# Two activation transposes moved from TensorE to transposing DMAs

## What is computed

```python
def _attn(x):
    xa = einsum('btc,dc->btd', x, W_attn + lora)          # q, k, v
    xa = (xa - xa.mean((0, 1))) * rsqrt(xa.var((0, 1)) + EPS) * bn_gamma + bn_beta
    q, k, v = split(xa, 3)
    y = softmax(causal(q @ k.T * scale)) @ v
    return (y @ W_proj.T) @ (W_proj + lora_proj).T
def _ffn(x):                                             # _bitlinear: quantised rows of x, ternary w
    return _bitlinear(silu(_bitlinear(x, w_gate)) * _bitlinear(x, w_up), w_down)
x = x + layernorm(_attn(layernorm(x)))
x = x + layernorm(_ffn(layernorm(x)))
```

## Time and profile before

| what | us |
|---|---|
| two timed runs of the kernel before | 7079.21 and 7239.78, median 7159.5 |
| the profiled execution's own time | 7071.24 |
| its span on the slowest core (core 6) | 7069.6 |
| spans of the eight cores | 7049.4 to 7069.6 |
| stage 1b, first load to last matmul | about 1801 to 2197 |
| stage 4b, first load of activations to the end | 6200 to 7070 |

### The profile page before, as it was taken

The page is one execution under the profiler, slowest core; times in us unless marked ns, Lnnn a source line. Parts: engine busy times, 40 slices in busy tenths (PEclk is TensorE's granted clock), DMA queues, the critical chain, the costliest instruction groups (busy, mean ns, idle before and its releaser), DMA issues.

```text
span 7069.6 us, 62509 instructions; the slowest of 8 cores (7049.4 to 7069.6 us)
## 1 busy us (share of the span) xinstructions
PE 4242.3 (60%) x18760; PEld 1818.9 (26%) x19100; DVE 2684.9 (38%) x3728; ACT 857.8 (12%) x1490; POOL 580.4 (8%) x2180
## 2 busy tenths in 40 slices
PE   5455555899895145555556531127777777567776
PEld 2111111223442022222222211113333333233333
DVE  2444444102443233333222234445555555542222
ACT  0222222000000001111111202111111111000000
POOL 0233333100000000000000000000000000000000
PEclk9988888999997567888888875558888888778888
DMA  4765555552222210000000023431111111222221
GB/s 138 221 192 192 191 192 192 167 177 84 72 87 72 82 35 30 30 30 23 23 23 20 21 94 126 146 125 36 36 42 39 36 36 36 92 96 75 84 84 69
DMA packets 244277, 626.46 MB, mean 89 GB/s; under 512 B 56376, under 2 KB 81000, under 8 KB 231592
## 3 DMA queue, kind: packets, MB, share of 16 engines
q1 hardware_dynamic: 243944, 622.44, 26.9%
HBM read 450.39 MB, written 171.97 MB: 88 GB/s over the span
## 4 chain that ended last, share of the span: by engine, by line
PE 45%; DVE 21%; DMA 14%; issue 10%; POOL 6%; ACT 2%; SPq 1%; DVEq 1%; POOLq 0%; another core or an unknown queue 0%; ACTq 0%
PE pall L1306 7%; PE pall L1198 5%; PE pall L680 5%; DMA xin<-x_all 5%; PE pall L1191 5%; PE pall L917 4%; PE pall L832 4%; PE pall L532 3%; DVE smalls L471 3%; DMA xt<-xnew_scr 2%; PE pall L937 2%; PE pall L538 2%; PE pall L955 2%; DMA vbn<-xa_scr 1%; POOL smalls L488 1%
## 5 line engine op out<-in xcount | busy, mean ns | idle before, releaser
L508 PE MATMUL pall<-lnx 128*128 128x512 bf16 x2007 | 606.7, 453 | 457.5 <-DVE lnx L491 454.2
L1191 PE MATMUL pall<-WgT,kqT 128*128 128x512 bf16 x1993 | 541.5, 417 | 255.3 <-DVE kqT L1180 252.1
L1198 PE MATMUL pall<-WuT,kqT 128*128 128x512 bf16 x2017 | 533.4, 409 | 98.5 <-DVE gu L1210 96.8
L1306 PE MATMUL pall<-WdT,gqT 128*128 128x512 bf16 x1990 | 507.7, 417 | 38.8 <-DVE gqT L1296 33.6
L508 PEld LDWEIGHTS pall<-lnx 128*128 128x128 bf16 x2048 | 204.3, 108 | 859.1 <-issue 725.6
L491 DVE TENSOR_SCALAR lnx<-xin,smalls 128x1024 bf16<-128x1024 f32 x256 | 208.2, 813 | 559.1 <-POOL smalls L488 559.1
L832 PE MATMUL pall<-Kfm,qfm 128*128 128x512 bf16 (+3 forms) x1136 | 286.1, 418 | 154.3 <-DVE qfm L816 153.3
L473 ACT ACTIVATE dummy1k<-xin 128x1024 f32<-128x1024 f32 x256 | 270.5, 1057 | 732.9 <-DMA xin<-x_all 732.8
L917 PE MATMUL pall<-Vtm,S_f 128*128 128x512 bf16 x1019 | 295.1, 434 | 100.8 <-DVE S_f L910 99.4
L1191 PEld LDWEIGHTS pall<-WgT,kqT 128*128 128x128 bf16 x2048 | 213.1, 105 | 533.2 <-issue 334.3
L680 PE MATMUL pall<-lnfm,WqkvT 128*128 128x512 bf16 x1504 | 343.2, 390 | 10.0 <-DVE lnfm L662 8.8
(11 more groups left out here) (213 smaller groups left out, 4630.2 us busy)
## 6 DMA issues: line engine op xcount, KB each, us to landing
xin<-x_all SPq DMA_DIRECT2D x256, 512.0 KB, 3.7
lnx_scr<-lnx SPq DMA_DIRECT2D x256, 256.0 KB, 2.2
lnb<-lnx_scr SPq DMA_DIRECT2D x256, 256.0 KB, 2.6
wstg<-w_gate SPq DMA_DIRECT2D x64, 512.0 KB, 3.6
wstg<-w_up SPq DMA_DIRECT2D x64, 512.0 KB, 4.0
gq_scr<-gq SPq DMA_DIRECT2D x32, 1024.0 KB, 4.8
gq<-gq_scr SPq DMA_DIRECT2D x32, 1024.0 KB, 6.1
xa_scr<-stg SPq DMA_DIRECT2D x48, 512.0 KB, 2.9
```

The lines of the kernel that those rows point to most:

```text
L508: s.add("pe", (lambda q, p=p, i=i, h=h, bi=bi, t=t: q.matmul(bank(bi), lnx[:, p, i * 128:(i + 1) * 128], lnx[:, p, h * 512:(h + 1) * 512], ...
L1191: s.add("pe", (lambda q, blk=blk, cj=cj, gb=gb, p=p: q.matmul(bank(gb), kqT[:, p, cj, :], WgT[:, cj, blk * 512:(blk + 1) * 512], start=(cj ...
L1198: s.add("pe", (lambda q, blk=blk, cj=cj, ub=ub, p=p: q.matmul(bank(ub), kqT[:, p, cj, :], WuT[:, cj, blk * 512:(blk + 1) * 512], start=(cj ...
L1306: s.add("pe", (lambda q, ds=ds, ic=ic, p=p: q.matmul(bank(ds), gqT[:, p, ic, :], WdT[:, ic, ds * 512:(ds + 1) * 512], start=(ic == 0), sto ...
```

## The change

The helper for DMAs gains a flag that makes the DMA transpose what it carries. In stage 1b the load `ld1b`, the 32 transposes and the 8 copies of a round are gone; 8 transposing DMAs per round, each 512 tokens x 128 channels of `lnx_scr` (128 KB), write `lnfm[:, lp, cj, :]` directly. They stand at the head of their own round, behind the six stores of the round before. In stage 4b the load `ldgq`, the 32 transposes and 4 copies of a round are gone; `ldgqT` issues 32 transposing DMAs per round, each 128 tokens x 128 channels of `gq_scr` (32 KB), into `gqT[:, p, ic, :]`. They stand where `ldgq` stood. All 8 DMAs of a round in stage 1b name the same written resource, `lnfm0` or `lnfm1`, and all 32 of a round in stage 4b name `gqT0` or `gqT1`.

```diff
-    def dma(self, eng, out, in_, reads=(), writes=(), name="dma"):
-        def emit(q, out=out, in_=in_):
+    def dma(self, eng, out, in_, reads=(), writes=(), name="dma",
+            transpose=False):
+        def emit(q, out=out, in_=in_, transpose=transpose):
+            if transpose:
+                return q.dma_start(out=out, in_=in_, transpose=True)
             return q.dma_start(out=out, in_=in_)
...
-    emit_ld1b(0)
     for st in range(8):
         lp = st % 2
         for cj in range(8):
-            tb = 2 + (cj % 2)
-            for i in range(4):
-                s.add("pe", (lambda q, i=i, cj=cj, tb=tb: q.transpose(
-                    bank_bf(tb)[:, i * 128:(i + 1) * 128],
-                    ln1b[:, i, cj * 128:(cj + 1) * 128], ident_bf)),
...
-            s.add("dve", (lambda q, cj=cj, lp=lp, tb=tb: q.tensor_copy(
-                lnfm[:, lp, cj, :], bank_bf(tb)[:, 0:512])),
-                reads=[PB[tb]], writes=[f"lnfm{lp}"], name=f"e1b{st}_{cj}")
-        if st + 1 < 8:
-            emit_ld1b(st + 1)
+            s.dma("sp", lnfm[:, lp, cj, :],
+                  lnx_scr[st * 512:(st + 1) * 512,
+                          cj * 128:(cj + 1) * 128],
+                  reads=[f"lnxs.{4 * st + i}" for i in range(4)],
+                  writes=[f"lnfm{lp}"], name=f"ldfm{st}_{cj}",
+                  transpose=True)
...
-    s.dma("sp", gq4[:, 0, :], gq_scr[0:128, :],
-          reads=["gqs.0"], writes=["gq40"], name="ldgq0")
-    transp4b(0)
+    def ldgqT(t):
+        p = t % 2
+        for ic in range(32):
+            s.dma("sp", gqT[:, p, ic, :],
+                  gq_scr[t * 128:(t + 1) * 128, ic * 128:(ic + 1) * 128],
+                  reads=[f"gqs.{t}"], writes=[f"gqT{p}"],
+                  name=f"ldgqT{t}_{ic}", transpose=True)
+
+    ldgqT(0)
     for t in range(NTO):
         if t + 1 < NTO:
-            s.dma("sp", gq4[:, (t + 1) % 2, :],
-                  gq_scr[(t + 1) * 128:(t + 2) * 128, :],
-                  reads=[f"gqs.{t + 1}"], writes=[f"gq4{(t + 1) % 2}"],
-                  name=f"ldgq{t + 1}")
+            ldgqT(t + 1)
         mm4b(t)
         tail4b(t)
-        if t + 1 < NTO:
-            transp4b(t + 1)
```

More of the change, by code:

```diff
@@ L654, in _build @@
         for cj in range(8):
-            tb = 2 + (cj % 2)
-            for i in range(4):
-                s.add("pe", (lambda q, i=i, cj=cj, tb=tb: q.transpose(
-                    bank_bf(tb)[:, i * 128:(i + 1) * 128],
-                    ln1b[:, i, cj * 128:(cj + 1) * 128], ident_bf)),
-                    reads=["R_xin0", "R_xin1", "R_xin2", "R_xin3", "ident_bf"],
-                    writes=[PB[tb]], name=f"t1b{st}_{cj}_{i}")
-            s.add("dve", (lambda q, cj=cj, lp=lp, tb=tb: q.tensor_copy(
-                lnfm[:, lp, cj, :], bank_bf(tb)[:, 0:512])),
-                reads=[PB[tb]], writes=[f"lnfm{lp}"], name=f"e1b{st}_{cj}")
-        if st + 1 < 8:
-            emit_ld1b(st + 1)
+            s.dma("sp", lnfm[:, lp, cj, :],
[4 more added lines that the diff above has]
+                  transpose=True)
         if dbg and st == 0:
```

## The result

The changed kernel takes 9055.5 us in the median of 11 runs, 8918 to 9215; the kernel before, measured again beside it, 7097.8 in the median of 10. The ratio is 1.263, 95% interval 1.258 to 1.267: slower by a quarter. The profiled execution took 8920.2 us, against 7071.2 of the one before, +1849 us. The eight cores lie between 8887 and 8919 us, where they lay between 7049 and 7070. In some executions the cores of one die run at a lower granted clock than the others; where that was so in an experiment, cores of the other die are named.

What follows compares the result with a forecast made beforehand. SP's chain of transposing round trips was taken to bound both stages, no longer PE, DVE or the clock: 7071.2 + 1905 (stage 4b) + 266 (stage 1b) = 9242, given as 9240 us, range 8500 to 10,400.

Steps and rivals of the forecast that it cites:

- d, a step of 32 KB: Stage 4b, one chained round trip of a 32 KB transposing DMA: 2.55 us, middle of plain 2.0 and piece-wise 3.1.
- residual, store and back, per round: Stage 4b, after a round's last transposing issue: residual's load, two DVE operations, store, next issue: 7.1 us.
- the last matmuls and the tail: End of stage 4b: last matmuls 13.6 us, 3.75 for low clock, 9.4 after the last PSUM reading: 27 us.
- stage 4b: SP's chain of 32 loads, then residual and store, sets a round of 86 us where it was 26.3: +1905 us.
- D, a step of 128 KB: Stage 1b, one chained round trip of a 128 KB transposing DMA: 4.6 us, middle of plain 2.5 and piece-wise 6.8.
- the low clock after the longer gaps: Stage 1b, the low clock may hold 7.5 us after a turn's gap, not 3: 2.2 us per turn.
- stage 1b: Eight 128 KB round trips exposed at the start and each turn, behind the stores: 294 - 28 = +266 us.
- The cover of the matmuls: Stage 4b: matmuls, 30 us even wholly at low clock, plus 8 us of tail fit into 79 us of next loads.
- B: Both stages: transposing costs nothing beyond the plain load, steps of 2.0 and 2.5 us, total 8560 us; 20%.
- D (about 30 ms): Both stages: transposition element by element in two-byte pieces, 17 us per 32 KB, about 30 ms; 4%.
- C: Both stages: SP's issue is slow as well, 1.4 us more: 11,410 us with the pieces, 10,040 without; 17%.
- A: Stage 4b: the 32 loads go out together at 0.33 us per issue, a round about 21 us, total 6905; 1%.

Runs made afterwards that it cites:

- experiment 2: The changed kernel with plain DMAs of the same slices in place of transposing ones, still chained, the transposition left out: span 8428.6 us.
- experiment 3: The changed kernel with one transposing DMA of 1 MB per round in each stage, in place of 32 and 8: span 6754.0 us, ratio 0.957 to the kernel before.
- experiment 1: The changed kernel with every slice of gqT and lnfm a resource of its own, so no transposing DMA waits for the one before: span 7803.6 us.
- experiment 10: Against experiment 9: stage 4b's transposing DMA of round t+2 issued right after round t's matmuls, ahead of residual's load and store: span 6639.1 us, ratio 0.939.
- experiment 7: The changed kernel, chains kept, with stage 1b's DMAs ahead of the stores and stage 4b's residual load ahead of the 32 DMAs: 8690 to 8703 us, cores 0 to 3.
- experiments 8 and 9: 8: against experiment 3, stage 1b's load ahead of stores, stage 4b's residual load ahead: 6720.2 us (core 3). 9: against 8, residual's load behind again: 6668.0 us.

## Why the prediction held, and where its sizes were off

The sign, the mechanism and the order of stages held: SP's chain, 1024 + 64 round trips, sets the end of both stages. The forecast of 9240 stands 184 above the median and 320 above the profiled execution, on which its terms rest: +2169 us were forecast and +1849 measured. Step by step:

| step | predicted | measured | worth |
|---|---|---|---|
| d, a step of 32 KB | 2.55 (2.0 to 3.1) | 2.33 | 994 x 0.22 = 219 us too much |
| residual, store and back, per round | 7.1 | 7.5 | 12 us too little |
| the last matmuls and the tail | 27 | 25.1 (8893.5 to 8918.6) | 2 too much |
| stage 4b | +1905 | +1698 | |
| D, a step of 128 KB | 4.6 (2.5 to 6.8) | 2.73 | 64 x 1.87 = 120 too much |
| the low clock after the longer gaps | 7 x 2.2 = 15 | 351.6 - 344.5 = 7 | 8 too much |
| stage 1b | +266 | +139 | |

**d.** Both of its halves were a little off, and in the same direction. The plain step is 1.85 us (experiment 2) where the chain of pA gave 2.0: that chain ran through TensorE and DVE between its loads, this one through SP alone. The transposition costs 0.48, where the middle of the two bounds gave 0.55. That this comes so close is luck: the 0.55 is half the price of pieces that the runs do not show, as D makes plain.

**D.** The step that failed is the assumption behind the upper end, that the transposition goes by pieces of 32 bytes at 16.7 ns of one DMA engine each. Four times the pieces cost 0.30 us more than a plain load and not 4.3. The counts of packets say the same (DMA of 7001 to 7053 us of the changed kernel, 23 issues to `gqT`, and of 7006 to 7058 us of experiment 2, 29 issues: packets, MB, share of 16 engines):

```profile
q1 hardware_dynamic: 3624, 0.74, 6.6%
...
q1 hardware_dynamic: 4106, 0.94, 7.8%
```

A transposing DMA of 32 KB has about 158 packets and a plain one 142; there are no 1024 packets for the assumed 1024 pieces. The term was sized from the packet price of a plain DMA and had no row of its own; with the 0.48 of d in its place D would have been 2.5 + 0.5.

**Stage 4b's round.** The order came out as written: L(t+1), residual, store, L(t+2), with L1337 waiting for the residual. What I had not seen is that a transposing DMA holds SP for 1.09 us, so that the residual's issue comes 1.14 us after the last one and not 0.45; its landing in 3.6 us instead of 3.8 made up for little of that. The cover of the matmuls was ample: they take 15.6 us of a round, and not for much of it at the low clock, as I had written, but for 3.1 us.

**Stage 1b.** The gap is 1.45 + 8 D as composed, and its mean of 23.3 gives the D of 2.73. The clock cost less than the 2.2 us a turn that I allowed: the matmuls of a round took 0.9 us longer in the mean than in the kernel before.

**What three rules of the Trainium skill give.** By "VectorE: DVE Perf Modes" of the Trainium skill, section on the three transpose paths, with its 1309 ns on top of the plain chain, d would have been 3.3; it is 2.33, and against the plain chain as measured here the transposition adds 0.48. By "Advanced Engine Details and Errata" of the Trainium skill, section X-Bar Transpose, it would cost nothing; the rows say 0.48 us per DMA of 32 KB and 1.1 us of SP instead of 0.32. What the runs bear out is the rule of "DMA: Bandwidth & Descriptors" of the Trainium skill, in its rules for kernel authors, to coalesce many small transfers because those under 64 KB are mostly overhead: experiment 3 moves what 32 DMAs of 32 KB moved in one, and its span is 2165 us below that of the changed kernel.

**The rivals.** B (8560, 20%) is refuted by experiment 2: the transposition has a price. Without it the same chains take 8429 us, below B's sum, since the plain step is 1.85 us and not 2.0. D (about 30 ms) is out by the measured step of 2.33 us. C was right that the issue is slower, by 0.77 us and not 1.4, but wrong on what that costs a chain: the step grows by 0.48 us in all, so part of the slow issue hides in the round trip; it comes to light in full when the chain is taken away (experiment 1). A was priced with the issue of a plain DMA, 0.33 us. With the true 1.29 its round is 48 us, so independent DMAs of 32 KB would not have ended on the other side. The way to a faster kernel was none of the rivals: fewer and larger DMAs.

## What to carry to other kernels

Before a DMA replaces on-chip work, count the round trips that its queue makes in a row: a scheduler that tracks a tile by one name turns n loads into a chain of n, here 2.3 us each, whatever the bandwidth. Make the slices resources of their own, or better, move the tile in one DMA: with 32 chained transposing DMAs of 32 KB a round takes 80 us, with 4 chained ones of 256 KB 22 us, and with one of 1 MB 14.7 us, nearly all of it matmuls. Put it on its queue ahead of what waits for this round's results (stage 1b, 334 us of matmuls and waits instead of 410), but not right behind a large plain load (stage 4b, 527 instead of 466).

## What the runs showed of the hardware

- A transposing DMA from SP holds SP for 1.10 us at 32 KB, 1.12 at 128 KB, 1.22 at 256 KB and, at 1 MB, for 5.4 to 5.6 in stage 4b and 4.8 to 5.2 in stage 1b (experiment 3), where a plain one of 32 or 128 KB holds it for 0.32 or 0.36. It lands after 2.2 us (32 KB), 2.6 (128 KB), 4.0 in stage 4b and 3.4 in stage 1b (256 KB) and 7.6 and 7.1 (1 MB, experiment 3; 8.3 in stage 4b of experiment 10, for a reason that was not looked into), against 1.7 and 2.3 for plain ones of the first two sizes and 6.1 for 1 MB.
- Right behind a plain store and a plain load of 512 KB a 32 KB transposing DMA takes 3.84 us, behind the store alone 2.49, behind another of its kind 2.25 (experiment 7); one of 1 MB lands in 9.9 us behind store and load and in 7.4 behind the store alone, and holds SP for 7.7 instead of 5.3 (experiments 8 and 9).
- After 63 us of rest, TensorE ran 8 matmuls in 3.1 us at 0.50 of the full clock, and the next 3 us were at 0.97. In the kernel before, a stretch of 7.5 us was at 0.50 in which transposes, waits and the first matmuls followed a rest of 6.35 us. These are the stretches of the changed kernel (start:end, us, busy us by engine, clock, DMA share, GB/s):

```profile
7057.30:7060.40 3.10, 3.06 (x8) 1.13 (x9) 0.69 (x1) 0.00 (x0) 0.00 (x0) 0.50 0.47 156
7060.40:7063.40 3.00, 3.00 (x15) 1.30 (x14) 1.35 (x2) 0.00 (x0) 0.00 (x0) 0.97 0.22 87
```
